# Writing out the turns of an attention block with two feed-forward halves: every engine's turns over eight sequences as straight code

## What is computed

```python
x = x + 0.5 * ffn(layernorm(x), w_gate, w_up, w_down)
x = x + attention(layernorm(x), Wq, Wk, Wv, Wo, bo)
x = x + 0.5 * ffn(layernorm(x), w_gate, w_up, w_down)

# ffn, with hidden size 768
h = silu(x @ wg.T) * (x @ wu.T)
return h @ wd.T
# attention, per head h of 16 channels
scores = q_h @ k_h.T / 4 - slope_h * abs(i - j)
return softmax(scores) @ v_h
```

## Time and profile before

| what | value |
|---|---|
| median of 3 runs | 909.1 us (907.73 to 913.88) |
| the profiled execution | 908.08 us |
| its span | 906.2 us |
| its mean granted clock on PE | 0.98 |
| PE matmul busy | 838.6 us, 93% |
| DVE busy | 661.3 us, 73% |
| ACT busy | 526.6 us, 58% |
| POOL busy | 425.9 us, 47% |

### The profile page before, as it was taken

How to read it: one execution, slowest core, us unless ns; L and a number is a source line. 1 busy time by engine, 2 the same in 40 slices (tenths; PEclk the granted TensorE clock), 3 DMA queues, 4 the chain that set the end, 5 groups by cost and what they waited for, 6 DMA issues and landing times.

```text
span 906.2 us, 15941 instructions
## 1 busy us (share of the span) xinstructions
PE 838.6 (93%) x4672; PEld 575.0 (63%) x4672; DVE 661.3 (73%) x1359; ACT 526.6 (58%) x745; POOL 425.9 (47%) x486
## 2 busy tenths in 40 slices
PE   3899998869999999999999999999999998999988
PEld 2788887735555665665665665565564447888877
DVE  5799997577677677677677677677678716777774
ACT  5344433415668658758758758768766684344443
POOL 0444433422635645645645644644644465344443
PEclk9999999967999999999999999999999999999999
DMA  9220000175383482482482482482482000010001
GB/s 382 83 66 7 0 0 2 38 197 140 83 223 69 106 221 50 103 222 48 98 222 53 95 225 53 93 225 56 91 228 54 3 1 2 25 46 23 23 23 48
DMA packets 37032, 84.48 MB, mean 93 GB/s; under 512 B 3746, under 2 KB 4770, under 8 KB 36818
## 3 DMA queue, kind: packets, MB, share of 16 engines
q1 hardware_dynamic: 36482, 83.45, 34.5%
q10 hardware_dynamic: 512, 0.53, 0.2%
HBM read 45.68 MB, written 38.87 MB: 93 GB/s over the span
## 4 chain that ended last, share of the span: by engine, by line
PE 76%; DVE 10%; DMA 5%; issue 4%; ACT 3%; POOL 1%; ACTq 1%; DVEq 0%; SPq 0%
PE ps L983 70%; DVE row_max L896 4%; DMA q_aug<-max_row 3%; PE ps L1034 2%; PE ps L995 2%; PE ps L1039 2%; DVE hid L784 1%; DVE xn L731 1%; ACT gated L590 1%; PE ps L1044 1%; DMA k_aug<-parts_scratch 1%; ACT stage L634 1%; DMA parts_scratch<-parts 1%; DVE w_max L846 1%; PE ps L1020 1%
## 5 line engine op out<-in xcount | busy, mean ns | idle before, releaser
L896 DVE TENSOR_REDUCE row_max<-ps 128x1 f32<-128x512 f32 x512 | 341.4, 688 | 125.3 <-PE ps L983 123.6
L678 ACT ACTIVATE probs<-ps 128x1024 f32<-128x1024 f32 x256 | 252.4, 1022 | 99.1 <-PE ps L983 88.3
L555 POOL TENSOR_TENSOR probs<-probs,diag 128x256 f32<-128x256 f32 x256 | 187.1, 733 | 231.7 <-ACT probs L678 231.3
L983 PE MATMUL ps<-k_aug,q_aug 96*128 96x512 f32 x512 | 221.5, 458 | 14.1 <-DVE row_max L896 6.8
L488 POOL TENSOR_TENSOR hid_r<-hid,hid_r 128x512 fp32r<-128x512 f32 x96 | 124.1, 1296 | 179.9 <-ACT hid_r L584 179.6
L983 PE MATMUL ps<-xnt,wgu_r 128*128 128x512 f32 x768 | 183.3, 395 | 14.5 <-DVE hid L784 7.0
L983 PEld LDWEIGHTS ps<-k_aug,q_aug 96*128 96x128 f32 x512 | 95.6, 194 | 146.4 <-DVE row_max L896 124.0
L983 PEld LDWEIGHTS ps<-xnt,wgu_r 128*128 128x128 f32 x768 | 142.9, 189 | 49.9 <-DVE hid L784 11.2
L983 PE MATMUL ps<-q_aug,k_aug 98*128 98x512 f32 x512 | 159.3, 404 | 7.3 <-DMA q_aug<-max_row 7.3
L983 PE MATMUL ps<-probs,v_aug 128*32 128x512 f32 x1024 | 137.1, 608 | 0.8 <-POOL probs L555 0.8
L590 ACT ACTIVATE gated<-ps 128x512 f32<-128x512 f32 x96 | 57.4, 598 | 116.6 <-PE ps L983 116.6
(11 more groups left out here) (62 smaller groups left out, 676.5 us busy)
## 6 DMA issues: line engine op xcount, KB each, us to landing
parts_scratch<-parts SPq DMA_DIRECT2D x128, 256.0 KB, 5.8
q_aug<-parts_scratch SPq DMA_DIRECT2D x32, 512.0 KB, 4.8
k_aug<-parts_scratch SPq DMA_DIRECT2D x32, 512.0 KB, 6.6
x_sb<-x_in SPq DMA_DIRECT2D x8, 512.0 KB, 12.7
x_out<-x_sb SPq DMA_DIRECT2D x8, 512.0 KB, 2.6
wgu_i<-w_gate_up SPq DMA_DIRECT2D x2, 768.0 KB, 5.9
k_aug<-k_rows_scratch SPq DMA_DIRECT2D x1, 1088.0 KB
w_att<-w_att SPq DMA_DIRECT2D x1, 1024.0 KB, 11.0
```

The source lines that it names most:

```text
L555: nc.gpsimd.tensor_tensor(tile, tile, diag[:, n * QH + 2 * pair:n * QH + 2 * pair + 2, :], ALU.mult).then_inc(fixed, 1)
L678: nc.scalar.activation(probs[:, kt % 2, 2 * pair:2 * pair + 2, :], ps[:, at:at + 2, :], ACT.Exp).then_inc(exp_done, 1)
L896: nc.vector.reduce_max(row_max[:, quad % 2, u % TT, u // TT:u // TT + 1], max_bank(b, tile)[0], mybir.AxisListType.X).then_inc(s1_used, 1)
L983: return nc.tensor.matmul(out, lhs, rhs, start=start, stop=stop, **k)
```

## The change

All turns on all engines are written out with plain integers. `turns` becomes a Python loop, the loop over phase a on DVE too, and there is no loop over a register left in the program. With that, the order on DVE of phase a becomes the order of phase c as well: the flag `early` goes, the statistics of sequence b + 2 are taken at the end of turn b, and those of sequence 1 in four instructions ahead of phase c.

```diff
         def turns(eng, body):
-            body(0)
-            with eng.Fori(1, B - 1) as b:
+            for b in range(B):
                 body(b)
-            body(B - 1)
...
-                early = w == 0
...
-                    if slots and f == (1 if early else 2):
+                    if slots and f == 1:
                         stats_ready(ready)
-                    if (then or w == 0) and f == ((3 if early else 4) if then else 0):
+                    if (then or w == 0) and f == (3 if then else 0):
                         wait(dve, s["turned"], 2 * b + 2 - 2 * w)
...
-                    if then and f < 2 and not early:
-                        ln_stats(0, b + 1, 2 * f)
-                        ln_stats(0, b + 1, 2 * f + 1)
-                    if slots and f == (1 if early else 2):
+                    if slots and f == 1:
                         ln_gather(slots)
-                    if slots and f in ((1, 2, 3) if early else (2, 3, 4)):
-                        ln_links(at, slots, (range(4), range(4, 9), range(9, LINKS))[f - (1 if early else 2)])
-                    if then and early and f in (3, 4, 5):
+                    if slots and f in (1, 2, 3):
+                        ln_links(at, slots, (range(4), range(4, 9), range(9, LINKS))[f - 1])
+                    if then and f in (3, 4, 5):
                         ln_apply(at, b + 1, ((0,), (1, 2), (3,))[f - 3])
-                    if then and not early and f in (4, 5):
-                        ln_apply(at, b + 1, (2 * f - 8, 2 * f - 7))
...
-                if early and not (isinstance(b, int) and b >= B - 2):
+                if b < B - 2:
                     for tile in range(TT):
                         ln_stats(0, b + 2, tile)
...
-            ffn_turn(0, 0)
-            with dve.Fori(1, B - 2) as b:
+            for b in range(B):
                 ffn_turn(0, b)
-            ffn_turn(0, B - 2)
-            ffn_turn(0, B - 1)
...
             turns(dve, turn)
-            turns(dve, lambda b: ffn_turn(1, b))
+            for tile in range(TT):
+                ln_stats(0, 1, tile)
+            for b in range(B):
+                ffn_turn(1, b)
```

## The result

The changed kernel takes 903.01 us (median of 7 runs, 902.50 to 903.34), the kernel before beside it 912.24 us (7 runs, 907.73 to 915.49). The ratio is 0.9901, 95% interval [0.9878, 0.9924]: 1.0% faster, where 910.5 us and no change had been forecast. Two things stand out beside the median. The kernel before spreads over 8 us, the changed one over 0.8. And the execution of the kernel before whose rows stand above took 908.08 us, near the fast end of its spread; the profiled one of the changed kernel took 903.27 us (span 901.5), so between the two traces there are 4.8 us to be found, and between the medians 9.2.

What follows compares the result with a forecast made beforehand. PE, busy 93% of the span, was taken as the bound. Attention 0, phase a -2.2, phase c -5.5 + 0.6, branches -3.0 and +10.7 + 1 made +1.6 on 908.08: 909.7, given as 910.5 for the median; range 899 to 921.

Steps and rivals of the forecast that it cites:

- The longer code, +10.7 + 1 us: PE's straight code: six new jump stalls, 14.3 us counted at three quarters, +10.7; jumps close to block ends, +1.
- Long branches that go, -3.0: PE's three long first-time branches at L1070 vanish, saving 2.33 + 0.41 + 0.3 us.
- Attention 0: Attention: register operations lie beside matmuls PE has queued, so removing them is worth 0.
- Phase a, -2.2: Phase a, turns 1 to 5: without register operations DVE's `xnt` comes earlier, saving 0.44 us each at the next turn's start.
- Phase c, -5.5: Phase c, turns 1 to 6: 1.20 us gap ahead of transposes goes, 0.28 us stall comes; 0.92 us saved each.
- Rival 3: Phase c's gain is absent: multiply 3 is as late as in phase a, its stall replacing the gap; 916 us, chance 0.1.
- Turn 0 of phase c, +0.6: Phase c's turn 0: division of the last heads now stands behind gather and links, costing 0.6 us, between 0 and 1.2.
- Rival 1: No PE jump stalls, as code comes one block ahead in time; 899.0 us, or 897.3, chance 0.2.

Runs made afterwards that it cites:

- the run with the link moved: Changed kernel with 4, 4 and 4 layer-norm chain steps behind DVE's multiplies 1, 2 and 3 in place of 4, 5 and 3: 898.38 us.
- all three steps moved: Changed kernel with one layer-norm step moved, phase c's turn 0 division ahead of the gather, and turn-end statistics behind `xnt`: 894.64 us.

## Why the prediction was wrong

- *The longer code, +10.7 + 1 us.* This step failed, and it alone gave the sum its sign. Six new long branches were forecast from a rule on where a jump stands in its block, which fitted 3 of 3 and 9 of 9; none came: all 32 took 0.205 to 0.414 us. What the three long branches shared was another thing: each lay behind a PE loop that had been left. The runs with one loop each show it for two; the third, in phase c's turn 1, goes when the loops before it go. That a long branch waits for an instruction fetch was read rightly; where such a wait arises was not. Without the step the sum is 909.7 - 11.7 = 898.0 us. The rule of the Trainium skill that was weighed there (Runtime: NRT & Kernel Launch, instruction fetch mechanics) comes out right for straight code: jumps over 190 to 260 instructions cost nothing that the spread lets one see. Where a branch was long, the traces show the fetch that the page speaks of; that it happens behind a loop that has been left is known from the runs.
- *Long branches that go, -3.0.* The two ahead of turn 7 of phase a and of phase c went for 2.5 and 0.5 us in the profiled pair, against 2.33 and 0.41 counted; the third lies in phase c's turn 1, below. But one execution was taken for all: at phase c's start the branch took 1.400 us in it, and 3.8 in another, with the clock falling behind it. This is where the median of before stands above its profile, and why the real gain is 9.2 and not 4.8 us. That the three runs shown spread over 6 us was in plain sight and not used.
- *Attention 0.* Right: 531.6 us from first to last step against 530.9 and, in the second profile of before, 531.5.
- *Phase a, -2.2.* The size is right, -2.6, the place only in part. The forecast was five turns of 0.44 us at the next turn's start. Turn 1 won nothing (20.18 and 20.12 us), turns 2 to 5 won 0.63 us each, 0.24 of them ahead of the transposes.
- *Phase c, -5.5.* The mechanism was right, the size not: -4.1 with the third long branch's 0.3 in it, so -3.8. Turns came out at 18.20 us in place of 17.93, as the wait on multiply 3 took 0.46 us a turn where 0.28 was counted. The interval from multiply 2 to 3, taken from phase a's turn 0, was right (2.98 us against 2.94), since it held the collision with POOL already. Wrong was that multiply 2 isn't late: it starts 6.00 us into the turn, not 5.83, behind a first link of 0.52 us in place of 0.17. Rival 3 named the right wait; against it was set that phase a's turns carry eight numbers, but with four numbers the wait was as long. It did not take the whole gain, as PE's other gap went.
- *Turn 0 of phase c, +0.6.* Too small: +1.7 us, since gather and links ahead of the division took 1.5 us in place of 1.1, and the division too ran into POOL's subtraction (1.25 us for its second instruction in place of 0.42). The lower clock behind the 2.00 us of waiting cost little: in the second profile of the changed kernel the same wait left the clock at 1.00, and the turn took 27.21 us in place of 27.36. The last turn's +0.8 us was overlooked altogether: it has no transposes, so it had no gap to lose, but it got the wait on multiply 3.
- *Rival 1 (899.0)* was the nearest: right on the jumps, 4 us low for the two points on phase c. That 903 lies inside the stated range of 899 to 921 is the width of the range; the forecast itself was 7.5 us off and said that nothing would change.

## What to carry to other kernels

A stall rule read from a dozen rows of one execution wants a second execution before it is priced, above all when the times themselves spread more than the terms of the sum. A gain worth taking in a looped kernel with jumps can be had by writing out only the engine that sets the pace: here PE alone gave two thirds. And where DVE runs a chain of tiny two-input steps beside POOL's big ones, the chain's cuts should be laid by POOL's timeline: moving one 0.16 us step won 4.6 us.

## What the runs showed of the hardware that was not expected

- After the end of a PE loop the first compare and branch over 48 unused matmuls took 3.3 to 3.9 us in eight cases of ten (1.4 to 1.5 in two at phase c's start), against 0.2 to 0.45 us in code written out (0.74, 0.75 and 0.93 us once each). Each long one ended 1.4 to 1.5 us after an instruction fetch had come in. Why the fetch is late behind a loop was not tried.
- A stall on PE can cost half as much again and more behind it. After 2.33 us of idling the next 2.95 us were granted 1.00, after 2.55 us 0.51. It isn't the length alone: with a loop in attention alone the clock was 0.53 behind only 2.31 us, and after 2.00 us of waiting for the division it was 0.68 in the changed kernel, while in the run with the link moved the sixteen matmuls behind the same 2.00 us took 3.90 us, at a clock of 1.00. Nor does all of it reach the end: behind the wait of 1.84 us that ends at 168.14 us the changed kernel's first profile has 0.70 for 3 us and its second 1.00, and the wait for `k_aug` that follows is 4.98 us in the first and 7.62 in the second.
- A DVE step of 0.16 us took up to 1.2 us beside a POOL subtraction; a multiply with one input from PSUM, and the gather, did not. With all three steps moved the chain still meets POOL in each turn, but where nothing waits for it.
